# A convolution stage moved from one-hot matmuls on TensorE to block additions on VectorE, with the buffers and waits around it rearranged

## What is computed

```
x = x + attn_a(layernorm(x), block_values, cols, rows)      # x: (2, 512, 256)

def attn_a(x, block_values, cols, rows):                    # 128 blocks of 64 x 64 x 16 taps
    xb = x.reshape(batch, n_block_row, bs, t)
    x_unfold = xb[:, cols].reshape(batch, n_blocks * bs, t)
    o = conv_general_dilated(x_unfold, W, padding=[(ks - 1, 0)], feature_group_count=n_blocks)
    y = zeros(...).at[:, rows].add(o)
```

## Time and profile before

| | |
|---|---|
| time, median of 3 runs | 879.3 us (879.21 to 879.4) |
| the profiled execution: its time | 878.04 us |
| its span, first to last instruction | 876.2 us |
| TensorE busy | 866.7 us (99%) |
| VectorE, ScalarE, GpSimd busy | 500.6, 420.7, 318.0 us |
| granted TensorE clock, mean | 1.00 |
| the convolution, in the trace | 0 to about 125 us of the span |

### The profile page before, as it was taken

One profiled execution on the slowest core, in us unless ns is written; L12 is line 12 of the kernel. 1 busy time (PEld: TensorE's weight loads), 2 busy tenths in 40 slices (PEclk: granted clock), 3 DMA queues, 4 the chain that ended last, 5 costly groups with the idle time before them and its releaser, 6 DMA issues. The chain is left out here.

```text
span 876.2 us, 16749 instructions
## 1 busy us (share of the span) xinstructions
PE 866.7 (99%) x5611; PEld 773.2 (88%) x5616; DVE 500.6 (57%) x1356; ACT 420.7 (48%) x978; POOL 318.0 (36%) x290
## 2 busy tenths in 40 slices
PE   9999999999999999999999999999999999999998
PEld 7999878888888888889989998998997888888887
DVE  5777747333333337887688678768876433333334
ACT  4522316334333344776477557647736433334332
POOL 5111013555565554132121213212112556555562
PEclk9999999999999999999999999999999999999999
DMA  8999311111111102000000000000002111111111
GB/s 338 360 389 402 116 54 56 55 47 42 54 36 54 54 18 75 1 26 6 32 1 24 36 0 24 0 0 1 1 1 73 37 54 37 53 54 36 54 36 49
DMA packets 25554, 61.01 MB, mean 70 GB/s; under 512 B 3298, under 2 KB 10916, under 8 KB 25508
## 3 DMA queue, kind: packets, MB, share of 16 engines
q1 hardware_dynamic: 23204, 47.82, 16.0%
q0 software_dynamic: 2304, 12.58, 3.7%
HBM read 59.35 MB, written 1.05 MB: 69 GB/s over the span
## 5 line engine op out<-in xcount | busy, mean ns | idle before, releaser
L983 DVE TENSOR_TENSOR f_h<-f_scaled,bank 128x512 f32<-128x512 f32 (+1 forms) x90 | 60.9, 676 | 179.4 <-POOL f_scaled L849 166.9
L764 ACT ACTIVATE f_h_hi<-f_h 128x512 fp32r<-128x512 f32 (+2 forms) x102 | 63.6, 624 | 187.3 <-DVE f_h L983 187.3
L849 POOL TENSOR_TENSOR f_scaled<-f_act,f_gate_rows 128x512 f32<-128x512 f32 x80 | 102.9, 1287 | 116.3 <-ACT f_act L757 115.9
L1083 PE MATMUL bank<-f_xt_hi,f_w_hi 128*128 128x512 f32 (+2 forms) x360 | 141.1, 392 | 0.5 <-ACT f_xt_hi L134 0.2
L1083 PE MATMUL bank<-f_xt_hi,f_w_lo 128*128 128x512 f32 (+2 forms) x360 | 141.4, 393 | 0.0
L1301 ACT ACTIVATE at_prob<-bank,at_sbias,at_qrs 128x512 f32<-128x512 f32 (+3 forms) x128 | 77.7, 618 | 72.4 <-DVE at_sbias L1494 72.4
L990 DVE TENSOR_TENSOR f_h_lo<-f_h,f_h_hi 128x512 fp32r<-128x512 f32 (+2 forms) x102 | 71.8, 704 | 70.7 <-ACT f_h_hi L764 70.2
L1083 PE MATMUL bank<-f_xt_lo,f_w_hi 128*128 128x512 f32 (+2 forms) x360 | 110.9, 390 | 0.0
L1096 PE MATMUL bank<-f_w_lo,f_h_hi 128*128 128x256 f32 (+1 forms) x352 | 99.6, 283 | 0.0
L1096 PE MATMUL bank<-f_w_hi,f_h_lo 128*128 128x256 f32 (+1 forms) x352 | 99.6, 283 | 0.0
L1096 PE MATMUL bank<-f_w_hi,f_h_hi 128*128 128x256 f32 (+1 forms) x352 | 99.3, 282 | 0.0
(11 more groups left out here) (225 smaller groups left out, 2044.0 us busy)
## 6 DMA issues: line engine op xcount, KB each, us to landing
cv_raw<-in_wconv SPq DMA_DIRECT2D x26, 512.0 KB, 7.6
cv_shared<-in_wtaps POOLq DMA_DIRECT2D x16, 768.0 KB, 8.1
f_wraw<-in_w SPq DMA_DIRECT2D x42, 256.0 KB, 2.6
xn<-in_wconv SPq DMA_DIRECT2D x14, 512.0 KB, 7.3
f_wraw<-in_w SPq DMA_DIRECT2D x42, 128.0 KB, 2.5
at_wraw<-in_wqkv SPq DMA_DIRECT2D x3, 768.0 KB, 4.4
at_oraw<-in_wo SPq DMA_DIRECT2D x4, 512.0 KB, 3.5
X<-in_x_tiles SPq DMA_DIRECT2D x2, 512.0 KB, 7.9
```

The source lines that it names most:

```text
L764: a.activation(h_hi[slot][0:rows, cols], h_f[half][0:rows, cols], ACT.Copy).then_inc(s["h_hi_done"], 1)
L849: g.tensor_tensor(scaled[half][:], act[half][:], gate_rows[:, half * HALF:(half + 1) * HALF], ALU.mult).then_inc(s["scaled_done"], 1)
L983: v.tensor_tensor(h_f[half][0:rows, cols], src[half][0:rows, cols], pu[half][0:rows, cols], ALU.mult)\
L1083: mm = t.matmul((pg, pu)[gu][half][0:out_rows, :], w, x, start=q == 0, stop=q == 3 * KH - 1)
```

## The change

Stage 4 leaves TensorE and goes to VectorE: NPE becomes 4 and ND 4. The one-hot sums of eight banks go, every addition handles 4 stages in place of 3 (a chunk of `wtaps` has 1 MB), and more blocks are dealt out per bank. A fourth added stage is split and multiplied at the end. Around it:

- banks: from bank 16 on the transfer of a bank waits until the bank three earlier has been summed (LEAD), since memory of two `raw` buffers is used again by others only later;
- the fp32 copies (`full`) and the rounded parts of the added stages overlap buffers that are dead at their time; stages 0, 2 and 3 share one copy, and ScalarE's first bank of a stage waits for the counts in FREED;
- the release of the rounded parts (`finish_products`) and the branch (`flagged_products`) are parted: the branch of stage st - 1 comes behind bank 1 of stage st, and each added stage has a branch of its own, behind its products for r = 0;
- `hold_open` puts two matmuls of zeros behind each bank of stages 2 and 3 and four before the last products of banks;
- three accumulators are closed together behind all products for r = 0;
- GpSimd clears `acc` in 8 parts and issues the first chunk before the second half of the powers.

```diff
-NPE, ND = 5, 3
-OB, DB, RING = 8, 8, 6
+NPE, ND = 4, 4
+OB, DB, RING, LEAD = 8, 8, 6, 3
...
-        raw += [sb(f"raw{i}", [P, CHUNK], F32)[:] for i in range(2, RING)]
+        raw += [sb(f"raw{i}", [P, CHUNK], F32)[:] for i in range(2, RING - 2)]
+        with nc.sbuf_tensor("cv_raw4", [P, CHUNK], F32) as raw4, nc.sbuf_tensor("cv_raw5", [P, CHUNK], F32) as raw5:
+            raw += [raw4[:], raw5[:]]
...
-        full = [sb(f"full{i}", [P, NW - NLOW, BS], F32) for i in range(2)]
...
+        full = [sb("full0", [P, NW - NLOW, BS], F32)]
+        with nc.sbuf_tensor("cv_full1", [P, NW - NLOW, BS], F32) as full1:
+            full.append(full1)
+        ws_hi.append(sb("ws_hi3", [P, NLOW, BS], F32R)[:])
+        ws_lo.append(sb("ws_lo3", [P, NLOW, BS], F32R)[:])
...
-        ZEROED = 4
+        ZEROED = 8
...
-        BANK_BLOCKS = ((5,) * 8, (5,) * 8, (6, 6, 6, 6, 6, 4, 0, 0))
+        FREED = {0: 1, 1: 2, 2: 4, 3: 7, NPE: 8, NST - 1: 9}
+        BANK_BLOCKS = ((7,) * 8, (8, 8, 8, 8, 8, 8, 10, 0))
...
-                    sp.wait_ge(s["summed"], c - RING + 1)
+                    sp.wait_ge(s["summed"], c - (RING if c < 2 * SB else LEAD) + 1)
...
-                    a.wait_ge(s["ws_free"], st + 1)
+                    a.wait_ge(s["ws_free"], FREED[st])
...
             g.wait_ge(s["flag_ready"], 1)
-            clear_sums(range(0, 3))
...
+            clear_sums(range(0, 4))
+            power(0)
+            blocks(0)
+            g.wait_ge(s["xn_ready"], GC)
+            clear_sums(range(4, 5))
+            power(1)
             g.wait_ge(s["xn_ready"], NT)
-            clear_sums(range(3, ZEROED))
...
+            clear_sums(range(5, ZEROED))
...
-            def finish_products(st):
+            def flagged_products(st):
                 t.wait_ge(s["ws_lo_done"], (st + 1) * SB)
                 with t.If(flag != 0):
                     t.wait_ge(s["ws_lo_done"], (st + 1) * SB)
...
+            def hold_open(count):
+                for _ in range(count):
+                    t.matmul(ps[4][:], zeros[:, 0:P], zeros[:], start=False, stop=False)
+
+            def finish_products():
+                t.matmul(ps[4][:, 0:1], zeros[:, 0:P], zeros[:, 0:1], start=False, stop=False)\
+                 .then_inc(s["ws_free"], 1)
...
             def convolve_last_banks():
+                hold_open(4)
                 t.wait_ge(s["ws_lo_done"], NPE * SB)
                 for c, r in LOW_PAIRS:
                     products(NPE - 1, c, r)
-                finish_products(NPE - 1)
+                finish_products()
+                flagged_products(NPE - 1)
...
             def convolve_added():
-                with t.If(flag != 0):
-                    t.wait_ge(s["added"], 2 + 2 * NBLK)
-                    for st in range(NPE, NST):
+                for st in range(NPE, NST):
+                    convolve_piece(st, 0)
+                    with t.If(flag != 0):
+                        t.wait_ge(s["added"], 2 + 2 * NBLK)
                         high_products(st)
-                for r in (2, 3):
+                for r in (2, 3, 0):
                     close(r)
...
+                for st in range(NPE, NST):
+                    convolve_piece(st, 1)
+                close(1)
...
                     if q == 1:
-                        t.wait_ge(s["ws_lo_done"], st * SB)
+                        flagged_products(st - 1)
                     for c, r in LOW_PAIRS[n:pace[q]]:
                         products(st - 1, c, r)
                     n = pace[q]
-                finish_products(st - 1)
+                    hold_open(2)
+                finish_products()
```

More of the change, by code:

```diff
@@ L158, in conv_phase @@
                          .rearrange("p (w o) -> p w o", w=NLOW) for i in range(2)] for part in range(2))
-        ws_hi += [sb(f"ws_hi{i}", [P, NLOW, BS], F32R)[:] for i in range(2, ND + 1)]
-        ws_lo += [sb(f"ws_lo{i}", [P, NLOW, BS], F32R)[:] for i in range(2, ND + 1)]
-        full = [sb(f"full{i}", [P, NW - NLOW, BS], F32) for i in range(2)]
+        ws_hi.append(sb("ws_hi2", [P, NLOW, BS], F32R)[:])
+        ws_lo.append(sb("ws_lo2", [P, NLOW, BS], F32R)[:])
+        full = [sb("full0", [P, NW - NLOW, BS], F32)]
[3 more added lines that the diff above has]
+        ws_lo.append(sb("ws_lo3", [P, NLOW, BS], F32R)[:])
+        sb("full1_rest", [P, NLOW, BS], F32)
         acc = sb("acc", [P, ND, NW, BS], F32)
@@ L203, in pair_index, with full_of @@
             return c * (NCB // 2) + row + (c >= NCB // 2) * (NW // 4) + (row >= NCB // 2) * (NLOW - NCB // 2)
+        def full_of(st):
+            return full[st == 1]
         def slot_of(st):
-            return st % 2 if st <= NPE else st - NPE + 1
+            return st % 2 if st < NPE else (0, 2, 3, 1)[st - NPE]
         def row_part(x, r):
@@ L264, in round_banks @@
                     sums, cols = ps[q % BANKS][:].rearrange("p (w o) -> p w o", o=OB), slice(q * OB, (q + 1) * OB)
-                    a.activation(full[slot][:, :, cols], sums[:, NLOW:NW, :], ACT.Copy)
+                    a.activation(full_of(st)[:, :, cols], sums[:, NLOW:NW, :], ACT.Copy)
                     a.activation(ws_hi[slot][:, :, cols], sums[:, 0:NLOW, :], ACT.Copy).then_inc(s["ws_hi_done"], 1)
@@ L288, in _ @@
                 for st in range(NPE, NST):
+                    if r == 0 and st == NST - 1:
+                        a.wait_ge(s["ws_free"], FREED[st])
                     round_sums(st, r)
@@ L310, in clear_sums, with blocks, power @@
                     g.memset(acc[:, :, q * NW // ZEROED:(q + 1) * NW // ZEROED, :], 0.0).then_inc(s["acc_zeroed"], 1)
-            g.wait_ge(s["flag_ready"], 1)
-            clear_sums(range(0, 3))
-            for b in range(B):
+            def blocks(d):
+                g.dma_start(raw_d[d % 3], ins["wtaps"][d].rearrange("p (n f) -> p n f", n=DB)).then_inc(raw_d_in[d % 3], 16)
+            def power(b):
                 part = slice(b * GC, (b + 1) * GC)
@@ L318, in _ @@
                  .then_inc(s["rstd_ready"], 1)
+            g.wait_ge(s["flag_ready"], 1)
+            clear_sums(range(0, 4))
[4 more added lines that the diff above has]
+            power(1)
             g.wait_ge(s["xn_ready"], NT)
-            clear_sums(range(3, ZEROED))
-            g.wait_ge(s["rstd_ready"], B)
-            for d in range(NDC):
-                if d in (1, 2):
+            clear_sums(range(5, ZEROED))
+            for d in range(1, NDC):
+                if d < 3:
                     g.wait_ge(s["xc_lo_done"], 4 * d)
-                if d >= 3:
+                else:
                     g.wait_ge(s["added"], 2 + 2 * DB * (d - 2))
-                g.dma_start(raw_d[d % 3], ins["wtaps"][d].rearrange("p (n f) -> p n f", n=DB)).then_inc(raw_d_in[d % 3], 16)
+                blocks(d)
             following["powers"](g, 0)
@@ L517, in high_products @@
                             if st < NPE:
-                                sums = full[st % 2][:, w - NLOW:w - NLOW + 2, :]
+                                sums = full_of(st)[:, w - NLOW:w - NLOW + 2, :]
                             else:
@@ L539, in convolve_last_banks, with convolve_piece @@
                     products(NPE - 1, c, r)
-                finish_products(NPE - 1)
+                finish_products()
+                flagged_products(NPE - 1)
+            def convolve_piece(st, r):
+                t.wait_ge(s["ws_lo_done"], piece_of(st, r) + 1)
+                for c in range(NCB // 2):
+                    products(st, c, r)
             def convolve_added():
-                with t.If(flag != 0):
-                    t.wait_ge(s["added"], 2 + 2 * NBLK)
-                    for st in range(NPE, NST):
+                for st in range(NPE, NST):
+                    convolve_piece(st, 0)
+                    with t.If(flag != 0):
+                        t.wait_ge(s["added"], 2 + 2 * NBLK)
                         high_products(st)
-                for r in (2, 3):
+                for r in (2, 3, 0):
                     close(r)
[L549 to L554, removed]
+                for st in range(NPE, NST):
+                    convolve_piece(st, 1)
+                close(1)
             def sum_and_convolve(st, pace):
```

20 lines of the change are left out of this document (11 added, 9 removed).

## The result

The changed kernel takes **888.0 us** (median of 4 runs) against 879.25: ratio 1.0098, 95% interval 1.0079 to 1.0118. It is slower, by 8.7 us where 9.6 were forecast. One of the four runs took 902.6; the ratio leaves it out, and the other three have a median of 887.4. The profiled execution took 887.4 us for a span of 885.6.

A forecast was written before the change was run, and what follows sets the result against it. TensorE, busy 99%, bounds the kernel before; after the change VectorE's last bank decides. TensorE's last close moves from 125.1 to 133.4, 8.3 us later, plus 1.3 for the clock: 9.6 on 879.3 gives 888.9 us, range 882.5 to 894.

The forecast's parts named there:

- VectorE's pace: VectorE's additions, widened from 128x96 to 128x128: 0.202 us from one to the next against 0.169, bounds 0.169 and 0.203.
- VectorE's end: VectorE's path through additions, bank subtractions, loads and waits: 99.6 without transfer waits, its last bank ready at 104.9.
- Transfers: Chunks and banks on the DMA queues: load per block unchanged, so VectorE's 5.0 us of chunk waits stay, bounds 0 and 10.
- the load three ahead: Bank loads for TensorE: waiting until three are left ahead instead of six costs nothing unless TensorE is over a bank late.
- The clock: TensorE after some twelve idle microseconds before the last products: a slow restart adds 1.3 us, bounds 0 and 1.3.
- the two ways weighed: TensorE's clock after a long wait: costs what the start costs, 1.3 (sum 9.6), or nothing, by the 1.08 gap (8.3).
- Branches exposed: Rival, 15%: four branches between TensorE's runs of added-stage products cost 1.0 us each, 4 more: 892.9.
- Keeps up: Rival, 9%: VectorE's additions keep the 128x96 pace at 128x128, last bank 8.3 us sooner: 879 to 874.
- Transfers limit more: Rival, 10%: chunks a third larger in the same ring of three double VectorE's waits to 10 us: 893.9.
- No gap and no late chunk: Rival, 10%: no clock loss on TensorE and no late chunk for VectorE, 3.3 us: 882.6.
- The cover of ScalarE's first copy: ScalarE's first copy of stage 3, behind the second bank's branch: 2 us of cover; if gone, lateness falls on VectorE's path.

The follow-up runs named there:

- both of VectorE's burdens off: Changed kernel, banks three ahead, with 256 bytes a partition loaded from the fourth chunk on and additions of 128x96 (stage 7 left out): 878.11 us, ratio 0.9988.
- the one-branch edit alone: Kernel before, with the products under the last bank stage's flag moved into the added stages' branch, so its last two branches are one: 877.80 us, ratio 0.9987.
- six ahead and 44 zeros: Changed kernel with banks six ahead and 44 matmuls with zeros in place of 4 before the last products: 885.11 us, ratio 1.0068.
- Small transfers alone: Changed kernel, banks three ahead, full-width additions, only 256 bytes a partition loaded from the fourth chunk on: 883.45 us, ratio 1.0044.
- Narrow additions alone: Changed kernel with banks six ahead and additions of 128x96 (stage 7 left out), all transfers kept: 883.74 us, ratio 1.0051.
- the one with five bank stages: Changed kernel without the move (five stages with TensorE's one-hot sums, three with VectorE), banks six ahead, no zeros: 879.42 us, ratio 1.0013.

## Why the prediction was right, and where not

*The forecast* held: VectorE became the bound, 888.0 against 888.9. Taking the move out (with six ahead and no zeros) gives 879.4, taking both of VectorE's burdens off 878.1. That the number is so near is in part luck: the next paragraphs show terms that were off by up to 7 us and terms that cancel.

*VectorE's pace* of 0.202 was right. That a bare subtraction of the same width on the same engine shows the price of the wider addition was the step that carried the forecast.

*VectorE's end* was forecast at 104.6 for the last subtraction and came at 103.44, by errors that cancel. Its additions began 0.8 later (39.65). Not all of that need be the change's: with the one-branch edit alone they begin at 39.54, and there the first eleven matmuls with zeros took 4.6 us, against 3.88; here they took 4.56. But with six ahead and 44 zeros they took 4.28, and the additions still began at 39.66, so the start doesn't explain it fully. The loads of pair numbers mostly cost 0.27 (48.02 to 48.49, less 0.20), not 0.45: 2.5 less. The chunks cost 4.0, not 5.0. These steps give 104.6 + 0.8 - 2.5 - 1.0 = 101.9, and 1.5 us are left. Most of them are small: an addition is 287 ns long and the next starts after 202, so each of the eight waits costs 0.085 more than its idle time (0.7), and three rows of additions ran slower than 0.202 each (those at 61.32, 67.71 and 95.25: 0.4).

*Transfers:* the forecast kept the 5.0 us, and 4.0 came. The four rows of VectorE's last bank show what each burden is worth. Small transfers alone brought the end forward by 4.6 us (103.44 to 98.81), which is all of the waits for chunks and a little more. Narrow additions alone gave 2.9 (102.85 to 99.92) and beside small transfers 4.6 (98.81 to 94.23), out of 8.3. So it is the narrower addition that can't be had for its full price: what VectorE saves, it waits for chunks and copies. By the times, narrow additions gave 3.5 us and small transfers 4.6 alone, and both together 9.9.

*The step that did not hold* is the one on the load three ahead: that TensorE "has time to spare there", so that it "costs nothing unless TensorE is late by over a bank". As a price it held here, since with six ahead the time was 887.21. The picture behind it did not: a bank took 7.8 us from issue to landing (the page's median; 7.6 in the kernel before), and TensorE waited 3.7 us for banks and lost clock from 77 to 84 us. Its idle time before the last products was 5.8 us where 12.6 were forecast, and 10.4 with six ahead. The sum stood only because all of this lay in front of VectorE's end. Where TensorE is the bound the same edit costs 37 us.

*The clock* was forecast to lose 1.3 behind the wait. It lost 1.9 in the profile (7.5 against 5.6 for the 24 products) and 2.1 by medians. The term was there and was too small; of the two ways weighed, the one that lets a long wait cost what a start costs was right. The Trainium skill (TensorE: Matmul & The Clock Gate, "What's actually happening") has activity release the clock again, and these products agree: by 107.8 they are 0.23 apart. The run without zeros does not: there TensorE was busy 9.81 and then 10.00 of 10 us, window after window, and stayed at 0.50 for some 60 us. The measurement decides: activity alone did not bring the clock back there.

*Branches exposed* (15%) is refuted: 887.5 without them. The 1.08 us gap goes when the two branches, which had a single small matmul between them, are made one. *Keeps up* (9%) is refuted by the 0.202. *Transfers limit more* (10%) did not happen at full width; at 128x96 it does, 7.4 us. *No gap and no late chunk* (10%): the run without late chunks still took 883.5, the one without the slow clock 885.1, so both costs are real.

*The cover of ScalarE's first copy* was rightly named: it holds in the changed kernel (no such wait behind 39.65) and is gone in two others, the one with both burdens off and the one with five bank stages, where 1.9 us of waiting appear.

## What to carry to other kernels

When work moves from a full engine to one that seems half idle, write down the second engine's whole path to its last result, instruction spacing and small loads included, and then what the first engine has left to do behind that result: here 14 us came off TensorE, and 24 more products came to stand behind VectorE's end. When two resources are nearly level, as VectorE and the transfers are here, test the relief of each alone and of both: 3.5 and 4.6 us alone, 9.9 together. Prefetch depth that is free while another engine sets the pace is not slack: measure it with the loaded engine as the bound before the buffers are given away.

## What was not expected

*A short wait can be followed by half the clock for a long time.* Waits of 1.2 to 1.7 us for a bank, in the stages of one-hot sums, were followed by 0.50 for 10 to 60 us of nearly uninterrupted work, in the kernel without zeros and in the kernel before with three ahead. In the changed kernel, with zeros behind each bank, such waits cost some 6 us of slow clock (78 to 84) or none (57.25), and with six ahead a wait of 1.6 us for VectorE cost none. The 36 matmuls with zeros looked like a cost of 7.8 us and are worth 4 to 6. Yet the gap of 1.08 us in the earlier trace rows, among the last products, cost no speed. What sets these cases apart is not shown.

*It can begin in the first stage.* So it did in the profiled execution of the kernel without branches, which took 900.2 us where that kernel's median is 887.5. Its timeline and windows of TensorE:

```profile
23.80 8.50 PE L520 MATMUL bank<-cv_onehot,cv_raw 128*128 128x64 f32 x44 [0.77 <-DMA cv_raw<-in_wconv]
```
```profile
30.00:40.00 10.00, 10.00 (x49) 10.00 (x48) 4.44 (x6) 4.93 (x9) 0.00 (x0) 0.50 0.78 266
```

A bank is 0.8 us late in the first stage, and the clock is down until about 52 us. Whether the early first chunk makes the bank late stays open.
